# Reordering VectorE, ScalarE, TensorE and GpSimd in the two convolution stages of a fused network block

## What is computed

```
x = x + conv0(ln_c(x))        # 4 experts of 3x3, top 2 per image by a router on the pooled image,
                              # group norm, Silu and a gate for each, plus a shared 1x1 branch
t = tokens(x); t = t + ffn0(ln_t(t))   # 8 experts, top 2 per token
x = x + conv1(ln_c(x))        # depthwise 3x3, taps computed per image and channel from the pooled image
t = tokens(x); t = ffn1(ln_t(t)) + t   # 8 experts, top 1 per token, capacity limited
```

## Time and profile before

| | before |
|---|---|
| median of three runs | 1973.59 us (1972.04 to 1975.29) |
| the profiled execution: time, span | 1975.22 us, 1973.5 us |
| mean granted TensorE clock | 0.926 of 2.4 GHz |
| TensorE busy | 1689.5 us (86%) |
| VectorE busy | 1473.1 us (75%) |
| ScalarE busy | 1015.7 us (51%) |
| GpSimd busy | 1052.3 us (53%) |
| second convolution's taps, first to last | 1243 to 1578 us |

### The profile page before, as it was taken

One profiled execution on the slowest core, in us unless ns is written; L12 is line 12 of the kernel. 1 busy time (PEld: TensorE's weight loads), 2 busy tenths in 40 slices (PEclk: granted clock), 3 DMA queues, 4 the chain that ended last, 5 costly groups with the idle time before them and its releaser, 6 DMA issues.

```text
span 1973.5 us, 39089 instructions
## 1 busy us (share of the span) xinstructions
PE 1689.5 (86%) x9187; PEld 947.3 (48%) x9188; DVE 1473.1 (75%) x5238; ACT 1015.7 (51%) x1725; POOL 1052.3 (53%) x1198
## 2 busy tenths in 40 slices
PE   2698899999999579999999991799899859999957
PEld 1444444454444335555555551455555534444447
DVE  5777778878778667777777773877777558888856
ACT  1434444435444357777777771265666435555524
POOL 1003455455464567777777775346675436666620
PEclk8698889989999789999999996899999969999989
DMA  8600111111110232222222214212220023222146
GB/s 269 187 11 32 46 41 45 45 44 45 45 49 26 74 105 84 77 77 84 78 78 82 78 45 107 64 45 82 76 71 24 26 82 88 84 78 72 35 128 214
DMA packets 180067, 149.09 MB, mean 76 GB/s; under 512 B 19303, under 2 KB 161823, under 8 KB 179961
## 3 DMA queue, kind: packets, MB, share of 16 engines
q1 hardware_dynamic: 153336, 98.05, 17.9%
q0 software_dynamic: 26624, 49.93, 7.5%
HBM read 76.00 MB, written 77.34 MB: 78 GB/s over the span
## 4 chain that ended last, share of the span: by engine, by line
PE 64%; DVE 14%; ACT 8%; issue 6%; DMA 3%; POOL 2%; ACTq 1%; SPq 1%; DVEq 0%; POOLq 0%
PE banks L780 15%; PE banks L781 15%; PE banks L782 14%; PE banks L775 10%; PE banks L994 5%; ACT work L1111 5%; ACT work L1207 2%; PE banks L1004 2%; PE banks L792 1%; DVE small L1532 1%; POOL slot_rows L645 1%; DMA wb_h<-ffn_rows 1%; DVE small L1507 1%; ACTq L1206 1%; DVE small L1503 1%
## 5 line engine op out<-in xcount | busy, mean ns | idle before, releaser
L666 POOL DMA_INDIRECT ffn_rows<-work x448 | 485.9, 1085 | 237.1 <-issue 167.0
L645 POOL DMA_INDIRECT slot_rows<-work,small x384 | 385.7, 1005 | 331.5 <-issue 155.2
L775 PE MATMUL banks<-small,work 128*128 128x128 f32 x1216 | 178.5, 284 | 141.4 <-ACT work L1111 110.7
L1919 DVE TENSOR_TENSOR work<-work 128x512 f16<-128x512 f32 x376 | 261.4, 695 | 12.6
L780 PE MATMUL banks<-work,wb_h 128*128 128x512 f16 x648 | 247.2, 382 | 17.3 <-DVE work L1956 12.8
L782 PE MATMUL banks<-work,wb_l 128*128 128x512 f16 x648 | 247.4, 382 | 0.0
L781 PE MATMUL banks<-work,wb_h 128*128 128x512 f16 x648 | 247.3, 382 | 0.0
L775 PEld LDWEIGHTS banks<-small,work 128*128 128x128 f32 x1216 | 144.1, 146 | 209.7 <-issue 105.6
L1935 DVE SCALAR_TENSOR_TENSOR work<-banks,small,work 128x512 f32<-128x512 f32 x216 | 161.4, 747 | 102.8 <-ACT work L1221 101.9
L780 PE MATMUL banks<-work,wa_h 128*128 128x512 f16 x576 | 233.2, 405 | 2.8 <-issue 2.8
L781 PE MATMUL banks<-work,wa_h 128*128 128x512 f16 x576 | 232.7, 404 | 0.0
(11 more groups left out here) (337 smaller groups left out, 3173.2 us busy)
## 6 DMA issues: line engine op xcount, KB each, us to landing
wa_l<-slot_rows SPq DMA_DIRECT2D x112, 264.0 KB, 2.8
work<-ffn_rows SPq DMA_DIRECT2D x32, 512.0 KB, 5.2
work<-in_x SPq DMA_DIRECT2D x16, 512.0 KB, 3.3
ffn_rows<-small SPq DMA_DIRECT2D x32, 256.0 KB, 3.9
out_image<-work SPq DMA_DIRECT2D x16, 512.0 KB, 3.1
ffn_rows<-work POOLq DMA_INDIRECT x448, 2.2
slot_rows<-work,small POOLq DMA_INDIRECT x384, 2.3
slot_rows<-small SPq DMA_DIRECT2D x17, 264.0 KB, 3.7
```

Of the source, the lines that this page charges most:

```text
L645: pool_e.indirect_dma_start(slots, bass.IndirectOffsetOnAxis(ap=slot_i[:, row_buffer(p, i, k), tt:tt + 1], axis=0), rows[row_buffer(p, i, ...
L666: pool_e.indirect_dma_start(dst, bass.IndirectOffsetOnAxis(ap=idg[old.v][:, qq, 0:1].bitcast(I32), axis=0), yt[old.u][:, qq, :], None, bou ...
L775: last = pe.transpose(dst[:, tt * P:(tt + 1) * P], x, ident)
L1919: dve.tensor_tensor(gl[i.u][:, j, :], g32[j], gh[i.u][:, j, :], ALU.subtract).then_inc(sem(p + "gl_done"), 1)
```

## The change

It changes orders and waits; apart from one image's sums, which go from GpSimd to VectorE, each engine has the operations it had. GpSimd, first convolution, and its start of the second:

```diff
@@ a_step, GpSimd @@
                     if some(nxt.b - 1):
                         pool_e.wait_ge(sem("A_logits_done"), nxt.b - 1)
+                    apart(pool_e)
+                    pool_e.wait_ge(sem("A_xt_done"), upto(nxt.b + 2, IMAGES))
                     pool_e.tensor_tensor(acc[nxt.u], act_o[of(0)], xcm[nxt.u], ALU.add).then_inc(sem("A_acc0"), 1)
@@ c_step, GpSimd @@
                 if isinstance(i.b, int) and i.b == -1:
-                    for k in range(3):
+                    pool_e.wait_ge(sem("C_stats"), 1)
+                    for k in range(1, 3):
                         sum_rows(Img(k // 2, k % 2))
```

TensorE. `positions` of the second convolution goes from behind tap 1 to behind taps 3 and 4:

```diff
@@ a_step, TensorE @@
                 if live(i, IMAGES):
-                    conv_half(i, 1, 1, regs, range(5))
+                    conv_half(i, 1, 1, regs, range(7))
                 if live(old, IMAGES):
                     pe.wait_ge(sem("A_acc2"), old.b + 1)
                     pe.wait_ge(sem("A_ntm"), upto(old.b + 3, IMAGES))
...
                     turn(tp, [acc[old.u][:, tt * P:(tt + 1) * P] for tt in range(TPI)]).then_inc(sem("A_tok_done"), 1)
+                if live(i, IMAGES):
+                    conv_half(i, 1, 1, regs, range(7, TAPS)).then_inc(sem("A_conv_done1"), 1)
+                if live(old, IMAGES):
                     a_logits(old)
-                if live(i, IMAGES):
-                    conv_half(i, 1, 1, regs, range(5, TAPS)).then_inc(sem("A_conv_done1"), 1)
@@ c_logits, TensorE @@
                 if some(i.b):
                     pe.wait_ge(sem("C_lg_read"), i.b)
+                    apart(pe)
+                    pe.wait_ge(sem("C_msum"), i.b)
@@ c_step, TensorE @@
                     taps(i, (1,))
-                if live(older, IMAGES):
-                    positions("C_", older)
...
                     taps(i, (3, 4))
+                if live(older, IMAGES):
+                    positions("C_", older)
```

ScalarE, second convolution:

```diff
@@ c_step, ScalarE @@
-                if isinstance(i.b, int) and i.b == -1:
-                    c_normal(nxt)
                 if live(old, IMAGES):
...
                     act.activation(cacc, pair[old.u], ACT.Copy, scale=wd_up[:, old.u, :]).then_inc(sem("C_conv_copied"), 1)
-                if live(older, IMAGES):
-                    route_exp("C_", older)
+                if live(nxt, IMAGES):
+                    c_normal(nxt)
...
                                    accum_out=pool[:, nxt.u, :]).then_inc(sem("C_inside"), 1)
+                if live(older, IMAGES):
+                    route_exp("C_", older)
+                if live(nxt, IMAGES):
                     act.wait_ge(sem("C_h_done"), nxt.b + 1)
...
-                if live(i + 2, IMAGES):
-                    c_normal(i + 2)
```

VectorE. `choose` also gets a `yield` after each of its six operations, so that it can be woven:

```diff
@@ a_step, VectorE @@
-                weave(has_old and group_affine(old, 2),
-                      has_nxt and token_stats(lambda tt: tp_tok[:, tt, :], 1e-6, image_stats, sem("A_image_stats")))
+                weave(has_nxt and token_stats(lambda tt: tp_tok[:, tt, :], 1e-6, image_stats, sem("A_image_stats")),
+                      has_old and group_affine(old, 2))
...
                 weave(has_old and accumulate(old, 2, 5),
                       has_older and route_place(older))
+                if isinstance(i.b, int) and 2 <= i.b <= 8:
+                    weave(direct_low(range(0 if i.b == 2 else i.b - 1, i.b)))
...
-                if isinstance(i.b, int) and i.b in (1, 2, 3):
-                    weave(direct_low(range(3 * i.b - 3, min(3 * i.b, 8))))
@@ c_step, VectorE @@
                 if isinstance(i.b, int) and i.b == -1:
+                    dst = tokens[:, 0:TPI, :]
+                    dve.wait_ge(sem("C_rows_loaded0"), 32)
+                    apart(dve)
+                    dve.tensor_tensor(dst, dst, ya[0], ALU.add).then_inc(sem("C_half_added"), 1)
+                    dve.wait_ge(sem("C_half_added"), 1)
+                    dve.tensor_tensor(dst, dst, yb[0], ALU.add).then_inc(sem("C_added"), 1)
...
-                if has_older:
-                    choose(older)
...
                     seen = token_moments(old, row_stats)
-                if has_nxt:
-                    dve.wait_ge(sem("C_inside"), nxt.b + 1)
-                    v = vpad[nxt.u][:, :, 1:H + 1, 1:W + 1]
-                    dve.tensor_tensor(v[:, 1], tp.rearrange("p (h w) -> p h w", h=H), v[:, 0], ALU.subtract).then_inc(sem("C_low"), 1)
...
                 weave((has_old or has_far) and scales(i, part, eps, seen),
-                      has_older and place_rows(older))
+                      has_older and choose(older))
+                if has_nxt:
+                    dve.wait_ge(sem("C_inside"), nxt.b + 1)
+                    v = vpad[nxt.u][:, :, 1:H + 1, 1:W + 1]
+                    dve.tensor_tensor(v[:, 1], tp.rearrange("p (h w) -> p h w", h=H), v[:, 0], ALU.subtract).then_inc(sem("C_low"), 1)
+                weave(has_older and place_rows(older))
```

More of the change, by code:

```diff
@@ L2056, in choose @@
                 dve.tensor_tensor(shifted, lg, gate1_b.to_broadcast([P, TPI, E]), ALU.add).then_inc(sem("C_lg_read"), 1)
+                yield
                 dve.wait_ge(sem("C_lg_read"), i.b + 1)
                 dve.tensor_reduce(s8[0], shifted, AX_X, ALU.max).then_inc(sem("dve_steps"), 1)
-                dve.wait_ge(sem("dve_steps"), L.step())
+                seen = L.step()
+                yield
+                dve.wait_ge(sem("dve_steps"), seen)
                 dve.tensor_tensor(shifted, shifted, bcast(s8[0], E), ALU.subtract).then_inc(sem("C_shifted"), 1)
+                yield
                 dve.wait_ge(sem("C_shifted"), i.b + 1)
                 dve.scalar_tensor_tensor(out=tmp8, in0=shifted, scalar=0.0, in1=desc8, op0=ALU.is_equal, op1=ALU.mult).then_inc(sem("dve_steps"), 1)
-                dve.wait_ge(sem("dve_steps"), L.step())
+                seen = L.step()
+                yield
+                dve.wait_ge(sem("dve_steps"), seen)
                 dve.tensor_reduce(s8[3], tmp8, AX_X, ALU.max).then_inc(sem("dve_steps"), 1)
-                dve.wait_ge(sem("dve_steps"), L.step())
+                seen = L.step()
+                yield
+                dve.wait_ge(sem("dve_steps"), seen)
                 dve.tensor_tensor(mask, tmp8, bcast(s8[3], E), ALU.is_equal).then_inc(sem("C_mask_ready"), 1)
+                yield
             def place_rows(i):
```

## The result

| | before | changed |
|---|---|---|
| median | 1972.82 us (1970.19 to 1975.29) | 1905.03 us (1902.60 to 1909.01) |
| ratio | | 0.9653 [0.9641, 0.9666] |
| span of the profiled execution | 1973.5 us | 1905.1 us |
| mean granted TensorE clock | 0.926 | 0.943 |
| TensorE, VectorE, GpSimd busy | 1689, 1473, 1052 us | 1669, 1461, 1047 us |

The change takes 68 us, 3.5%. Lines of the changed kernel lie 2 to 27 further down than before: the transposes are line 778 (was 775), GpSimd's sums 682, 699 and 702 (680, 697, 700), the last group statistic 1718 (1713), the positions 803 (800), the copy of a convolution 1280 (1276), the scales' first and last operation 2048 and 2053.

What follows compares the result with a forecast made beforehand. TensorE was taken as the bound, held up by holes before its transposes and, in the first convolution, stretches at 1.2 GHz. First convolution -50.5, second -11.5: -62 us, from 1973.6 to 1912, range 1874 to 1950.

Steps and rivals of the forecast that it cites:

- (e): First convolution: low parts one a step, two steps with high parts at 73 us, -11 us; very first steps -1.
- (f): Second convolution's start: VectorE adds the first image's rows, GpSimd's sums wait for its statistics; first taps at 1234.0, -9.3 us.
- (g): Second convolution, chooser woven with the scales: steps without GpSimd's sums at 18.9 us; first three -8.7, last three -6.5.
- (h): Second convolution's ten steps between: GpSimd's sums lock the weave, a loop of 22.0 us a step, +13 us.
- (a): First convolution: GpSimd's sum waits for the next image's transposes; last group statistic takes 0.2 us, token statistics start 1.8 earlier.
- (b): First convolution: two more taps before TensorE's transposes, router products behind the last taps; 1.98 us hole closes, 1.1 to spare.
- (c): First convolution: without the hole TensorE's clock stays at 2.4 GHz, 2.55 us a step; bounds all or none.
- (d): First convolution: 31.2 us plus 1.1 of unplaced waits, 32.3 a step, bounds 31.2 and 34.3; eleven steps -38.5 us.
- rival 2: First convolution keeps slow stretches or VectorE's serial work takes TensorE's place: 34.3 a step, 22 us more, 1934; chance 0.27.
- Rivals 1: Rival 1: GpSimd's sums miss the weave in the second convolution, ten steps at 18.9, 31 us less, 1881; chance 0.16.
- Rival 3: Second convolution: VectorE's diagonals hold GpSimd's scatters 3 us in each of ten steps; 25.0, 30 us more, 1942; chance 0.06.
- Rival 4: Slower: the second convolution's new 3 us hole drops TensorE to 1.2 GHz and it stays; 2002 with six steps; chance 0.05.

Runs made afterwards that it cites:

- after_pe_undone: Changed kernel with TensorE's first-convolution order undone (five taps before the transposes, router products right behind them): 1922.97 us, 0.9732 of the kernel before.
- logits_only: Kernel before with only the first convolution's router products moved behind the last taps, transposes still behind the fifth tap: 1952.96 us, ratio 0.9891 to before.
- low_only: Kernel before with only the first convolution's low parts made one a step: 1960.93 us, ratio 0.9930 to before.
- sums_apart_all: Changed kernel, second convolution's GpSimd sums behind the fourth scatter, first step's sum held for three of the first image's diagonal groups: 1879.57 us, 0.9519 of before.

## Why the prediction came out right, point by point

1912 was forecast, 1905 measured: -68 us for -62. The total is nearer than its halves: -61.5 us for -50.5 in the first convolution and -4.7 for -11.5 in the second, misses of 11 and 7 us that point opposite ways. So the mechanisms were right, and that the sum came within 7 us is in part luck. The forecast's own steps, by the traces (the last 2 us came behind the second convolution):

| step | forecast | measured |
|---|---|---|
| first steps of the first convolution (e) | -1 | -4.8 |
| two steps with high parts (e) | -11 | -16.0 |
| eleven steps (a to d) | -38.5 | -40.7 |
| start of the second convolution (f) | -9.3 | -5.1 |
| its first three steps (g) | -8.7 | -8.6 |
| ten steps (h) | +13 | +16.0 |
| last three (g) | -6.5 | -7.0 |

- **(a), the lock.** Right: 0.22 us for 2.03. Taking the wait out again costs 11 to 12 us.
- **(b), the hole.** Closed, but with 0.2 us to spare and not 1.1: in one step of the changed kernel the image is written at 259.85 us and the transposes start at 260.06. Only 1.3 of the 1.8 us won at the statistics reach ScalarE's normalisation, which starts 7.4 us behind the tokens' transposes (249.56 to 256.96) for 8.7 before (417.85 to 426.53). after_pe_undone shows the same: 1.0 us of hole where the sum left 0.2. Without the two taps, and with the narrow products back behind the hole, most steps keep their 32.1 us and the clock goes in some.
- **(c), the clock.** Right: all of it came back. The row that I leaned on, a hole of 1.80 us with full products before the narrow ones, would not have carried it alone: logits_only makes the first convolution like it, with the hole of 2.0 us kept, and that only halves the time at 1.2 GHz (41 us for 78). The hole had to close too.
- **(d), 32.3 a step.** 32.1. The 1.1 us of waits that I couldn't place are about 0.8: 2.3 us before transposes, 2.6 of issue and 3.4 before the small product at line 905, in ten steps. The bound of 34.3, which rival 2 uses too, doesn't follow from its terms: 31.2 and 2.55 make 33.8, and 34.9 with the 1.1 us of waits.
- **(e), mis-sized, 9 us too small.** I kept a hole of 3.2 us for ScalarE's high parts; it was 1.4 and 1.5, and the clock stayed. I had put all 4.25 us on the path, but some 2.5 us of it fell into time in which ScalarE otherwise idles before its Silu (2.2 us in a later step): Silu starts 8.1 us behind the tokens' transposes with high parts and 6.3 without. low_only shows the other half: the low parts alone are worth 14 us, 9 of them in the two steps and 2 in the steps ahead of these.
- **(f), mis-sized.** -5.1 for -9.3. The first statistics came as worked out, 13.6 us behind the first row load for 22.1 before (-8.5 for -8.4). Behind them I missed two locks: GpSimd's sum of the fourth image starts at 1170.68 and holds the tap-weight operations (2.87 for 0.22 us and 5.00 for 3.02). sums_apart_all takes these away and gets 4.4 us back at the first taps. How much of the start reaches the end is open.
- **(g)** right within 0.5 us, steps of 19.0 without sums included.
- **(h), right in cause, near in size.** The sums fell on the weave, as worked out, and moving them away brought 23 us. But I had it as one loop of 22.0 in every step; it is long and short steps, three of them at 19.0, and I hadn't counted the clock: some 37 us at 1.2 GHz in these ten steps (10.2 us three times, 6.8 once) and 19 lost. So 22.3 beside 22.0 is in part luck: the holes are 1.8 to 2.5 us in seven steps, where 3 in each were forecast, and the clock makes up for it.
- **Rivals 1 and 2** didn't come: the sums met the weave in seven of ten steps, and the first convolution ran at PEclk 1.00.
- **Rival 3.** The scatters beside the diagonals took 0.97 to 1.03 us, as elsewhere: the rows were right against descriptors being held. The same page of the Trainium skill, SBUF — State Buffer, section Who interferes with whom, says that a two-port operation and a GpSimd operation exclude each other. With GpSimd's sums the diagonals behave so, 8.15 us for 3.02; the trace doesn't name the mode that they run in.
- **Rival 4**, slower, was closer than its 0.05 looks: stretches did come, but ended after 10.2 us and the clock never stayed down. With the positions left in place they come in every step and the kernel is slower than before. Its first half was right, that the new hole drops the clock; what kept the time away was the one move that I gave no price of its own.

## What to carry to other kernels

Before an operation is moved off another engine's short operations, write out what lies where it will land: here the sums went from one lock into another, and a place one scatter (1.3 us) further on was worth 15 us. The price of a TensorE hole depends on what stands behind it too: here the same 2.0 us hole cost half as much time at 1.2 GHz once full products came before the narrow ones. When a producer is moved later in a step, move its consumer in the same edit.

## What the runs showed of the hardware beyond that

- A float16 multiplication by a scalar per partition on VectorE, one large operand, is locked by GpSimd's sums like an operation with two operands: eighteen took 3.02, 5.00 and 8.15 us, by how much of the sums lay on them; a float32 one of 128x9 took 2.87 for 0.22.
- TensorE's clock answers to more than the length of a hole: 2.0 us and then narrow products, slow in every step; 2.0 us with full products behind the transposes, in six of eleven; 1.0 with narrow products behind, in four of eleven; 0.7, or 1.4 to 1.9, with full products behind, in none of the steps looked at.
